# Degrees of a graph kernel: counts added up on GpSimd, one f32 product per range instead of one f16 product per step

## The reference

```python
h = (feat - mean) * rsqrt(var + EPS) * gamma + beta
a_in  = segment_sum((h @ W_in  + b_in)[src]  * iw[:, None], dst, num_segments=N)
a_out = segment_sum((h @ W_out + b_out)[dst] * ow[:, None], src, num_segments=N)
# ... gates of layer 0 ...
deg = segment_sum(ones(E), dst, num_segments=N)      # layers 1, 2 and 3
agg = segment_sum(x[src] + e_msg, dst, num_segments=N) / maximum(deg, 1.0)[:, None]
```

## Time and profile before

| | us |
|---|---|
| median of 3 runs | 3228.72 |
| the profiled execution | 3224.97 |
| its span, first to last instruction | 3223.1 |
| PE busy in the span | 2547.6 (79%) |
| DVE busy | 1684.7 (52%) |
| ACT busy | 1255.8 (39%) |
| POOL busy | 822.0 (26%) |
| the degree products (L947, 500 columns), records | 150 of mean 0.379 |

### The profile page before, as it was taken

How to read it: one execution, slowest core, us unless ns; L and a number is a source line. 1 busy time by engine, 2 the same in 40 slices (tenths; PEclk the granted TensorE clock), 3 DMA queues, 4 the chain that set the end, 5 groups by cost and what they waited for, 6 DMA issues and landing times.

```text
span 3223.1 us, 36451 instructions
## 1 busy us (share of the span) xinstructions
PE 2547.6 (79%) x14593; PEld 1397.2 (43%) x14593; DVE 1684.7 (52%) x1858; ACT 1255.8 (39%) x2535; POOL 822.0 (26%) x611
## 2 busy tenths in 40 slices
PE   0561047777777777889999799998999989999896
PEld 0320023333333333445444444555555665545543
DVE  3442579999999996555555545102122234132314
ACT  0138057677777613666666513001011121111203
POOL 3000467777777752223222200000000000000000
PEclk9795579999999999999999999999999999999897
DMA  9999853333333324777777543323323224333242
GB/s 371 405 386 409 269 110 49 59 58 59 59 59 53 44 17 153 236 245 245 247 237 242 144 124 75 124 72 106 105 81 96 96 78 127 109 111 105 84 148 67
DMA packets 220444, 472.29 MB, mean 147 GB/s; under 512 B 85174, under 2 KB 132942, under 8 KB 220044
## 3 DMA queue, kind: packets, MB, share of 16 engines
q1 hardware_dynamic: 140885, 426.39, 39.1%
q0 software_dynamic: 57360, 0.92, 4.9%
q10 hardware_dynamic: 22023, 42.59, 4.1%
HBM read 319.59 MB, written 150.22 MB: 146 GB/s over the span
## 4 chain that ended last, share of the span: by engine, by line
PE 48%; DMA 13%; POOL 11%; SPq 10%; DVE 8%; issue 6%; ACT 4%; ACTq 0%; DVEq 0%; POOLq 0%
PE psum L1050 25%; POOL cell_mat L515 11%; PE psum L998 11%; DMA cell_mat<-ROW 10%; SPq L356 10%; PE psum L930 6%; ACT Q L664 3%; DVE AR L1342 2%; DVE Q L1407 2%; PE psum L944 2%; DMA Q<-cell_mat 1%; PE psum L1067 1%; ACT Q L655 1%; DMA cell_mat<-SA 1%; PE psum L1077 1%
## 5 line engine op out<-in xcount | busy, mean ns | idle before, releaser
L1050 PE MATMUL psum<-FR 125*128 125x500 f16 (+1 forms) x4200 | 822.3, 355 | 20.8 <-DVE FR L1461 20.8
L515 POOL DMA_INDIRECT cell_mat<-ROW x391 | 622.9, 1593 | 534.7 <-DMA cell_mat<-SA 327.5
L900 PE MATMUL psum<-AR,Q 128*128 128x500 f16 (+1 forms) x2737 | 592.8, 356 | 183.7 <-DVE AR L1342 179.8
L1342 DVE TENSOR_SCALAR AR<-Q,ROW 128x3125 f16<-128x3125 f16 x391 | 721.2, 1900 | 7.0 <-PE psum L900 0.5
L1050 PEld LDWEIGHTS psum<-FR 125*128 125x128 f16 x4200 | 387.7, 98 | 428.9 <-issue 44.3
L900 PEld LDWEIGHTS psum<-AR,Q 128*128 128x128 f16 x2737 | 237.4, 98 | 455.2 <-DVE AR L1342 182.3
L1488 DVE SCALAR_TENSOR_TENSOR Q<-psum,small,ROW 128x1000 f32<-128x1000 f32 (+1 forms) x42 | 48.2, 1147 | 712.6 <-PE psum L1050 712.5
L1407 DVE SCALAR_TENSOR_TENSOR Q<-Q,small 125x1000 f16<-125x1000 f32 (+1 forms) x175 | 251.1, 1438 | 178.7 <-ACT Q L664 178.5
L524 POOL CAST Q<-Q 128x500 f16<-128x500 f32 (+1 forms) x175 | 173.8, 994 | 487.7 <-DMA Q<-cell_mat 472.2
L998 PE MATMUL psum<-wl,Q 128*125 128x256 f32 (+1 forms) x1100 | 286.8, 401 | 5.7 <-ACT Q L721 3.0
L944 PE MATMUL psum<-Q,FR 125*128 125x500 f16 (+1 forms) x1050 | 233.9, 360 | 60.2 <-DVE Q L1407 58.4
(11 more groups left out here) (278 smaller groups left out, 2324.1 us busy)
## 6 DMA issues: line engine op xcount, KB each, us to landing
cell_mat<-SA SPq DMA_DIRECT2D x39, 3000.0 KB, 31.7
Q<-cell_mat SPq DMA_DIRECT2D x150, 750.0 KB, 5.3
FR<-count_mat SPq DMA_DIRECT2D x180, 625.0 KB, 3.8
AR<-cell_rows ACTq DMA_DIRECT2D x47, 640.0 KB, 4.2
count_mat<-Q SPq DMA_DIRECT2D x150, 125.0 KB, 4.9
AR<-in_edge_attr SPq DMA_DIRECT2D x13, 960.0 KB, 4.9
Q<-in_edge_attr SPq DMA_DIRECT2D x48, 256.0 KB, 4.3
cell_mat<-ROW POOLq DMA_INDIRECT x391, 3.1
```

The costliest lines, as they stand in the source:

```text
L515: pool.indirect_dma_start(out=cell_mat, out_offset=bass.IndirectOffsetOnAxis(ap=at[c % VALS][:, k:k + 1], axis=0), in_=vals[c % VALS][:, k ...
L900: last = pe.matmul(a, own_attr, onehot[t % 3][:, t0:t0 + nt], start=t == 0, stop=t == ET - 1, skip_group_check=True)
L1050: last = pe.matmul(a[:, hh, 0:w], parts[:, c, t, f], slot(m, j)[0:P, i_, :], start=t == 0 and c == 0, stop=t == NT - 1 and c == 1, skip_gr ...
L1342: dve.tensor_scalar(onehot[t % 3], iota16, dst_c[:, t:t + 1], None, ALU.is_equal).then_inc(S["onehot_ready"], 1)
```

## The change

POOL adds up the counts itself. After its cast of a step it waits for that cast, and in step 0 of a range copies the 125 rows into a new f32 sum (`count_sum`, L529), in every other step adds them to it (L532). The copy of a new range waits until PE has read the sum of the range before (`deg_summed`). PE no longer multiplies in each step; one product in f32 per range, ones by the sum (`degree_of`, L960), takes its place. It stands in PE's list where the in-products of the next range's step 0 begin, behind the one-tile out-products. DVE's `degree` waits for that product (`deg_summed`) and no longer for the range's last step (`step_done`). POOL's cast drops its wait for PE's step n-4. In the changed kernel the lines read: PE out-products L938, in-products L951, transposes L968; DVE low part L1421, degree L1411 to L1415.

```diff
+        count_sum = Q[0:P, q2 + 4 * COLS:q2 + 5 * COLS]
-        ones16 = tiny(64).bitcast(F16)
+        one = tiny(1)
...
                 if n >= 4:
                     pool.wait_ge(count_stored[n % 4], 16 * (n // 4))
-                    pool.wait_ge(S["step_done"], n - 3)
                 pool.tensor_copy(counts[n % 4][:, 0:w], ...).then_inc(S["count_ready"], 1)
+                pool.wait_ge(S["count_ready"], n + 1)
+                if t == 0:
+                    if r:
+                        pool.wait_ge(S["deg_summed"], r)
+                    pool.tensor_copy(count_sum[:, 0:w], counts[n % 4][0:P, 0:w]).then_inc(S["count_added"], 1)
+                else:
+                    pool.wait_ge(S["count_added"], n)
+                    pool.tensor_tensor(count_sum[:, 0:w], count_sum[:, 0:w], counts[n % 4][0:P, 0:w], ALU.add).then_inc(S["count_added"], 1)
...
-                if t == 0:
-                    if r:
-                        pe.wait_ge(S["in_read"], r)
-                        pe.wait_ge(S["deg_read"], r)
+                if t == 0 and r:
+                    pe.wait_ge(S["in_read"], r)
+                    degree_of(r - 1)
...
-                pe.wait_ge(S["count_ready"], n + 1)
-                return pe.matmul(deg_acc[:, 0:w], ones16, counts[n % 4][0:P, 0:w], start=t == 0, stop=t == NT - 1, skip_group_check=True)
+                return last
+
+            def degree_of(r):
+                w = RANGES[r][1] * P
+                pe.wait_ge(S["count_added"], (r + 1) * NT)
+                if r:
+                    pe.wait_ge(S["deg_read"], r)
+                pe.matmul(deg_acc[:, 0:w], one.to_broadcast([P, 128]), count_sum[:, 0:w], start=True, stop=True, skip_group_check=True).then_inc(S["deg_summed"], 1)
...
+            degree_of(NR - 1)
             out_part(pending)
...
                 if t == 0 and r:
-                    dve.wait_ge(S["step_done"], n)
+                    dve.wait_ge(S["deg_summed"], r)
                     degree(r - 1, False)
-            dve.wait_ge(S["step_done"], NS)
+            dve.wait_ge(S["deg_summed"], NR)
             degree(NR - 1, False)
```

More of the change, by code:

```diff
@@ L271, in build_gnn @@
                  "abs_done eq_done before_done claim_done free_ready w_ready sum_done ded_read vals_ready attr_hi attr_lo onehot_ready attr_done s_ready "
-                 "hi_ready lo_ready count_ready step_done turned in_read deg_read out_mm out_added deg_staged "
+                 "hi_ready lo_ready count_ready count_added deg_summed step_done turned in_read deg_read out_mm out_added deg_staged "
                  "first_scale gates gate_used mv_ready std_ready norm_ready agr_ready agg_ready piece_used "
@@ L943, in in_part @@
                     for q, (c, d) in enumerate(((0, 0), (0, 1), (1, 0))):
-                        pe.matmul(in_acc[:, hh, 0:w], feat[0][:, t, c, f], split[n % 3][:, d, 0, 0:w],
+                        last = pe.matmul(in_acc[:, hh, 0:w], feat[0][:, t, c, f], split[n % 3][:, d, 0, 0:w],
                                   start=t == 0 and q == 0, stop=t == NT - 1 and q == 2, skip_group_check=True)
-                pe.wait_ge(S["count_ready"], n + 1)
-                return pe.matmul(deg_acc[:, 0:w], ones16, counts[n % 4][0:P, 0:w], start=t == 0, stop=t == NT - 1, skip_group_check=True)
+                return last
[5 more added lines that the diff above has]
+                pe.matmul(deg_acc[:, 0:w], one.to_broadcast([P, 128]), count_sum[:, 0:w], start=True, stop=True, skip_group_check=True).then_inc(S["deg_summed"], 1)
             def turns(n):
@@ L1179, in _ @@
             dve.memset(be_last[:, :], 0.0)
-            dve.memset(ones16, 1.0)
+            dve.memset(one, 1.0)
             dve.memset(src_f, float(N))
```

## The result

The changed kernel takes 3248.72 us (median of 4, 3245.98 to 3250.42), the kernel before 3229.34 in the same comparison (median of 4): 19.4 us more, a ratio of 1.006 with a 95% interval of 1.0042 to 1.0077. The profiled execution has a span of 3244.2 us where 3223.1 stood, 21.1 more.

The account below looks back on a forecast made before the run. Within the steps the chain was taken to go round between engines, PE not simply full. -9 + 15 + 2 + 13 = +21 us on the profiled 3224.97 gave 3246, or 3250 against the median; range 3233 to 3284.

Parts of the forecast that it names:

- Degree products that go: In the steps on PE: 175 degree products leave, worth their 1.5% share of the 604 us chain, -9 us.
- DVE waits for the f32 product: At six changes of range: DVE's degree begins 2.5 us later behind PE's f32 product, +15 us.
- The seventh product: At the end of the stage: the last f32 product, of 125 columns, costs some 0.2 us.
- POOL's copy waits for the same product: At six changes of range: POOL's late additions run during two DVE low parts, 0.3 us each, +2 us.
- The additions: In 30 groups: a 1.25 us POOL addition delays DVE's critical low part by 0.89 us in half of them, +13 us.
- Additions that never meet: Rival, in the groups: additions never meet DVE's critical low part, so +8 us, 3237; chance 0.2.
- A long addition: Rival, on POOL: an addition takes 1.72 us or above and meets every group, +53 us, 3282; chance 0.2.
- Faster: Rival: the 2.5 us at changes of range cost nothing, additions find gaps, 9 us remain gained, 3220; chance 0.05.

Follow-up runs that it names:

- the fills: The changed kernel with each POOL addition replaced by two fills of the sum with ones, which read nothing from SBUF: 3239.95 us.
- the additions alone: The kernel before with POOL's copy and additions put in, their sum read by nobody: 3240.20 us, against 3229.52 before.
- the degree moved away alone: The kernel before with DVE's degree put ahead of the last full group's addition at a change of range: 3200.32 us, against 3229.12 before.
- the product earlier: The changed kernel with PE's f32 product moved ahead of the one-tile out-products: 3234.42 us, against 3229.52 for the kernel before.

## Why the prediction was right, step by step

- *Degree products that go, -9.* Measured by themselves -7.1, with an interval from -4.5 to -11 that holds both the 9 and the 30 x 0.21 = 6 that I set aside; the 6 lies nearer. The share of the chain also holds products outside the groups: 9 us are 43 products of 0.21, and 30 of them are those of the groups.
- *DVE waits for the f32 product, +15.* Right in place and size: the degree begins 2.56 us later at each change, where 2.5 was forecast, the changes are 15.5 us longer, and moving the product alone takes 14.3 us back. The product measured 0.91 on the chain, 0.84 was read from the earlier trace rows. The seventh product was priced wrongly: I gave it 0.2 at the end of the stage for its own length, but DVE's last degree, its last addition and the last out-products wait for it in a row, and the end is 1.8 us longer.
- *POOL's copy waits for the same product, +2.* Nothing: that SP hides the late counts was right, and the late additions, for which the 2 stood, cost nothing here, since without any additions the changes are as long (147.5). The two low parts at 1445.67 were disturbed (3.87 together, 3.00 without additions), but at that place it didn't matter.
- *The additions, +13.* Alone they cost 10.7 in the median and 12.6 in the groups; in the changed kernel 9.5 in the median, but only 30 x (13.96 - 13.74) = 6.6 in the groups. That one excludes the other stands in the rows at 1397.17, and that it comes from what GpSimd reads is shown by the fills. The duration was below my 1.25: 1.13 undisturbed. The estimate of 1.10 worked out from the Trainium skill (GPSIMD Engine Reference, section 3.1, Elementwise) was nearer. That half of the groups would be met was right (15 of 30 in the changed kernel are longer than 13.90, the others lie between 13.70 and 13.88), but such a group is 0.47 us longer than 13.70 on average, and not 0.89. The place was only half right. I had the addition slip in just ahead of the critical low part; the rows at 1397.17 show an addition holding back the low part before it, that one holding back a cast, and the cast holding back the critical one.
- *Sum.* By these measurements -7 + 15 + 0 + 10 = +18, against +21 predicted and +19.4 measured. By place, in the two profiles: products and additions were forecast at -9 + 13 = +4, and the groups changed by +0.3; the changes were forecast at 15 + 2 = +17 and grew by 15.5; for the last range and the two ends of the stage nothing stood in the sum, and they grew by 4.9. So the mechanism at the changes was right, and the agreement to 1.3 us (3248.72 against 3250) is in good part luck: the 5 us by which the groups and the changes fell short were made up at the stage's ends and in the last range.
- *The rivals.* "Additions that never meet" is refuted by the additions alone. "A long addition" fell with 1.13. "Faster" needed something later than the degree at a change; the degree moved away alone gains 28.8 us, so nothing there was near it. That PE's clock falls behind a change is so, and after the change it falls at all five changes to a full range, as the prediction held possible; but it falls at four of them with the product earlier too, where the six changes are within 1.1 us of before.
- *Left open.* The last range is 2.9 us longer, of which the prediction had nothing. Without additions it is 1.9 longer, and between the experiments it moves from 26.5 to 30.5 without a pattern that I can name; one profile each doesn't settle it.

## What to carry to other kernels

Work moved to GpSimd isn't free because GpSimd is idle: if it reads SBUF it can shut out VectorE instructions that have two SBUF inputs, so look in the trace at what those instructions do while GpSimd's run, before adding more. When many small products are gathered into one at the end, look at who waits for the last of them and what stands ahead of it in its engine's list; and ask of every piece of work at such a place whether it could stand ahead of a wait instead of behind it, which here was worth more (28.8 us) than the whole change cost (19.4).

## What the runs showed that was not expected

An addition on GpSimd that started 0.03 us behind a VectorE low part (1397.20 against 1397.17) still went first and ran undisturbed (1.14), so where two starts lie that close, their order in the trace doesn't tell which instruction goes first. And 288 fills of 500 columns on GpSimd, 157.6 us together, left VectorE's low parts where they were (1.588 against 1.586).
